# Graph attention hops: head rows loaded as a broadcast, scores spread by a bf16 product, tail scores added on the vector engine

## What is computed

```python
head, tail = (edge_index[0], edge_index[1])          # src, dst
rel_e = relation_emb[edge_type]
def agg(emb):
    a_input = jnp.concatenate([emb[head], emb[tail]], axis=-1)
    h = a_input @ fc_w.T + fc_b
    e = jnp.sum(h * rel_e, axis=-1)
    e = jnp.where(e > 0, e, LEAKY_SLOPE * e)          # slope 0.2
    m = jax.ops.segment_max(e, head, num_segments=N)
    ex = jnp.exp(e - m[head])
    denom = jax.ops.segment_sum(ex, head, num_segments=N)
    w = ex / denom[head]
    agg_emb = jax.ops.segment_sum(emb[tail] * w[:, None], head, num_segments=N)
    return agg_emb + emb
for _ in range(2):
    emb = agg(emb)
    nrm = jnp.sqrt(jnp.sum(emb * emb, axis=-1, keepdims=True))
    emb = emb / jnp.maximum(nrm, EPS)
```

## Time and profile before

| | us |
|---|---|
| median of 3 runs | 8037.34 |
| lowest and highest | 8023.26, 8038.31 |
| the profiled execution | 8036.36 |
| its span, first to last instruction | 8034.5 |
| POOL busy | 5792.3 (72%) |
| PE busy | 5700.0 (71%) |
| DVE busy | 4755.5 (59%) |
| ACT busy | 2380.1 (30%) |

### The profile page before, as it was taken

The page is one execution under the profiler, slowest core; times in us unless marked ns, Lnnn a source line. Parts: engine busy times, 40 slices in busy tenths (PEclk is TensorE's granted clock), DMA queues, the critical chain, the costliest instruction groups (busy, mean ns, idle before and its releaser), DMA issues. The chain is left out here.

```text
span 8034.5 us, 180792 instructions
## 1 busy us (share of the span) xinstructions
PE 5700.0 (71%) x46174; PEld 3902.5 (49%) x46175; DVE 4755.5 (59%) x24755; ACT 2380.1 (30%) x4713; POOL 5792.3 (72%) x5647
## 2 busy tenths in 40 slices
PE   0991699999001477778777767777777777588885
PEld 0110111111000377667677766777767667466664
DVE  6898655555001466666666666666666666555555
ACT  2000000000000244454444444545454445122221
POOL 0888877777777577777777747777777777277775
PEclk9995899999555687887888877887787888588888
DMA  2992577886001211212211221111212122233332
GB/s 68 307 309 63 151 244 244 244 244 212 4 4 21 62 53 53 53 53 53 53 53 53 53 48 53 53 53 53 53 53 53 53 53 53 34 69 69 69 68 55
DMA packets 375221, 721.44 MB, mean 90 GB/s; under 512 B 210770, under 2 KB 259945, under 8 KB 325885
## 3 DMA queue, kind: packets, MB, share of 16 engines
q10 hardware_dynamic: 76307, 411.51, 15.5%
q0 software_dynamic: 180560, 257.90, 14.7%
q1 hardware_dynamic: 118298, 51.38, 2.8%
HBM read 693.09 MB, written 19.44 MB: 89 GB/s over the span
## 5 line engine op out<-in xcount | busy, mean ns | idle before, releaser
L1108 POOL DMA_INDIRECT rows<-tab_d,stage_idx x3264 | 3090.3, 947 | 1100.8 <-issue 972.0
L214 POOL DMA_INDIRECT rec_d<-stage_rec,stage_row x1600 | 1955.4, 1222 | 673.1 <-issue 664.6
L424 PE MATMUL ps_gate<-ring,h_sb 128*1 128x512 f32 x3072 | 1486.3, 592 | 0.2 <-issue 0.2
L1150 PE MATMUL ps_x<-a_split,hot_t 128*128 x9792 | 577.8, 198 | 782.2 <-DMA rows<-tab_d,stage_idx 780.6
L1252 DVE SCALAR_TENSOR_TENSOR picked<-iota_f,typ_e,ps_x 128x50 f32<-128x50 f32 x3264 | 679.8, 264 | 685.6 <-PE ps_x L1153 680.5
L1161 PEld LDWEIGHTS ps_g<-rows,prob 128*128 128x128 f32 x6528 | 1070.3, 235 | 9.7 <-ACT prob L1196 8.5
L1161 PE MATMUL ps_g<-rows,prob 128*128 128x65 f32 x6528 | 1022.0, 310 | 2.7 <-ACT prob L1196 2.7
L1452 POOL DMA_INDIRECT y_rows<-y_d,stage_src x768 | 735.6, 958 | 368.6 <-issue 218.9
L1150 PEld LDWEIGHTS ps_x<-a_split,hot_t 128*128 128x128 bf16 x9792 | 464.0, 104 | 1014.1 <-issue 967.3
L1220 DVE CUSTOM_DVE_ANT_0 masked<-lower,ps_s 128x512 f32<-128x512 bf16 x816 | 561.7, 688 | 550.2 <-ACT lower L1190 420.9
L1188 ACT ACTIVATE hot_t<-ps_hot 128x512 bf16<-128x512 bf16 x816 | 487.1, 597 | 1271.8 <-PE ps_hot L1141 1258.4
(11 more groups left out here) (289 smaller groups left out, 7822.9 us busy)
## 6 DMA issues: line engine op xcount, KB each, us to landing
ring<-w_ih ACTq DMA_DIRECT2D x192, 1024.0 KB
ring<-w_hh ACTq DMA_DIRECT2D x192, 1024.0 KB
rows<-tab_d,stage_idx POOLq DMA_INDIRECT x3264
rec_e<-list_lo_d SPq DMA_DIRECT2D x216, 128.0 KB
rec_d<-stage_rec,stage_row POOLq DMA_INDIRECT x1600
y_rows<-y_d,stage_src POOLq DMA_INDIRECT x768
rec_d<-blank ACTq DMA_DIRECT2D x1, 3584.0 KB, 32.5
rec_e<-rec_d SPq DMA_DIRECT2D x1, 3584.0 KB, 11.2
```

Source lines behind the costliest of these rows:

```text
L214: pool.indirect_dma_start(out=rec_d, out_offset=bass.IndirectOffsetOnAxis(ap=stage_row[:, h, j:j + 1], axis=0), in_=stage_rec[:, h, j, :], ...
L424: mm = pe.matmul(ps_gate[:, s, :], lhsT=h_sb[:, kc:kc + 1], rhs=ring[:, pc % RING, q, :], start=(kc == 0), stop=(kc == KC - 1))
L1108: pool.indirect_dma_start(out=rows[:, h * 4 + g, k, :], out_offset=None, in_=tab_d[hop], in_offset=bass.IndirectOffsetOnAxis(ap=stage_idx[ ...
L1150: pe.matmul(ps_x[:, p, k * R:(k + 1) * R], lhsT=hot_t[:, p, k * P:(k + 1) * P], rhs=a_split[:, ds(bb, 1), j, :].rearrange("p a r -> p (a r)"),
```

## The change

All of it is in the hops and in what feeds them.

- **Head rows.** The position of each edge's head in its block, `lo`, is stored in device memory as bf16, one row of 512 per group (`lo_d`; new in the block of stage 2: an ACT copy `lo_rows` and one DMA). In a hop SP loads each group's row, broadcast to 128 partitions (`lo_wide`, 128 KB). DVE compares it with the partition's number: one instruction of 512 columns gives `hot_t`, another gives `lower`. The four `hot` instructions, PE's `turn_hot` and both ACT copies go.
- **Scores spread.** DVE splits each score in three bf16 parts in a zero-filled tile of 128 columns (`s_parts`). PE turns it (one bf16 transpose), ACT copies 128 columns (`s_rows`), and PE multiplies with constants `pick_k`, four bf16 products, in place of four f32 transposes.
- **Tail scores.** PE's f32 product L1153 goes. DVE adds `ps_x` and the tail scores in `rows` (`x_sum`, 200 columns), and `picked` reads `x_sum`. Now DVE, and not PE's `scores`, waits for `rows`.
- **Running maximum.** `m_old` is copied first and is the start value of the maximum; the factor for new sums is 1, so `acc` is updated by one instruction.
- **Lags** are 1, 2, 3 and 4 in place of 1, 2 and 3. `PER_GROUP` counts DVE's own waits, 12 for 8.
- In stage 2 `lo_e` is turned where `only_lo` was; `node_a` is replaced by `part_f` in the last stage.

```diff
@@ stage 2
-                sp.wait_ge(kept_rdy, CHUNKS // 2)
+                sp.wait_ge(kept_rdy, CHUNKS // 2 + 1)
+                sp.dma_start(lo_d.rearrange("g (k e) -> (g k) e", k=KT).rearrange("(c t) e -> t c e", t=P), lo_rows[:]
+                             ).then_inc(list_st, 16)
                 sp.dma_start(tile_d[0:T1].rearrange("(c p) e -> p c e", p=P), by_tile[:].rearrange("p c v e -> p c (v e)")
                              ).then_inc(tile_st, 16)
...
-                dve.scalar_tensor_tensor(out=only_lo[:], in0=rec_e[:, :, 3], scalar=-float(B_LO), in1=rec_e[:, :, 0],
-                                         op0=ALU.mult, op1=ALU.add).then_inc(to_turn, 1)
+                dve.tensor_copy(lo_e[:], rec_e[:, :, 0]).then_inc(to_turn, 1)
...
+                for k in range(KT):
+                    link(dve.tensor_copy(pick_k[:, k, :], ident_f[:, k:k + 1].broadcast_to([P, P])))
+                for j in range(1, 3):
+                    for k in range(KT):
+                        c = j * KT + k
+                        link(dve.tensor_tensor(pick_k[:, k, :], pick_k[:, k, :],
+                                               ident_f[:, c:c + 1].broadcast_to([P, P]), ALU.add))
...
+                act.wait_ge(kept_rdy, CHUNKS // 2)
+                act.activation(lo_rows[:], by_tile[:, :, 0, :], ACT.Copy).then_inc(kept_rdy, 1)
@@ hop, SP
+                        def head_rows(g, u):
+                            wait_tick(sp, tick, lo_in, g * 16)
+                            wait(sp, lower_rdy, g - 7)
+                            sp.dma_start(lo_wide[:, u % 8, :], lo_d[ds(g, 1), :].broadcast_to([P, GE])).then_inc(lo_in, 16)
+
+                        def round_of(it, last=False):
+                            for u in range(8):
+                                if not last or u + LO_AHEAD < 8:
+                                    head_rows(it * 8 + u + LO_AHEAD, u + LO_AHEAD)
+                                if not last and u % 4 == 3:
+                                    half(it + 1, u // 4)
@@ hop, PE
+                        def turn_scores(g, p):
+                            wait(pe, score_rdy, g + 1)
+                            wait(pe, s_kept, g)
+                            pe.transpose(ps_turn[:, 0:P], s_parts[:, p].rearrange("p j k -> p (j k)"), ident_b[:]
+                                         ).then_inc(s_turned, 1)
...
-                                mm = pe.transpose(ps_s[:, p, k * P:(k + 1) * P],
-                                                  score[:, p, k:k + 1].broadcast_to([P, P]), ident_f[:])
+                                mm = pe.matmul(ps_s[:, p, k * P:(k + 1) * P], lhsT=pick_k[:, k, :], rhs=s_rows[:, p, :],
+                                               start=True, stop=True)
...
                         def scores(g, p, u, bb):
-                            wait(pe, landed[u], (g - u) * 8 + 64)
...
-                            mm = pe.matmul(ps_x[:, p, 0:KT * R], lhsT=ident_f[:], rhs=rows[:, u, :, SC:SC + R],
-                                           start=False, stop=True, skip_group_check=True)
@@ hop, ACT
-                                act.activation(hot_t[:, p, :], ps_hot[:, 0:GE], ACT.Copy).then_inc(hot_t_rdy, 1)
-                                act.activation(lower[:, p, :], ps_hot[:, 0:GE], ACT.Copy, bias=-BIG, scale=BIG
-                                               ).then_inc(lower_rdy, 1)
+                                act.activation(s_rows[:, q, :], ps_turn[:, 0:P], ACT.Copy).then_inc(s_kept, 1)
@@ hop, DVE
+                                link(dve.tensor_scalar(m_old[:, p:p + 1], m_of, 1.0, None, ALU.mult))
...
+                                wait(dve, lo_in, i * 16 + 16)
+                                wait(dve, x_rdy, i - 1)
+                                dve.tensor_scalar(hot_t[:, u % 2, :], lo_wide[:, u % 8, :], part_f[:], None, ALU.is_equal
+                                                  ).then_inc(hot_t_rdy, 1)
+                                dve.tensor_scalar(lower[:, u % 4, :], lo_wide[:, u % 8, :], part_f[:], -BIG,
+                                                  ALU.not_equal, ALU.mult).then_inc(lower_rdy, 1)
...
+                                wait(dve, landed[(u - 1) % 8], (g - (u - 1) % 8) * 8 + 64)
                                 wait(dve, x_rdy, g + 1)
+                                link(dve.tensor_tensor(x_sum[:], ps_x[:, q, 0:KT * R].rearrange("p (k r) -> p k r", k=KT),
+                                                       rows[:, (u - 1) % 8, :, SC:SC + R], ALU.add))
```

207 lines of the change are left out of this document (96 added, 111 removed).

## The result

The changed kernel takes **8066.15 us** in the median (8064.8 to 8068.7), the kernel before 8037.5 beside it: ratio 1.0038, 95% interval 1.0026 to 1.005. It is slower by 29 us, more than the 0.2% that can be told from no change. The forecast was 8058 (8032 to 8150), with "slower" at 0.50 and "the same" at 0.46.

A forecast was written before the change was run, and what follows sets the result against it. POOL's back-to-back gathers, one group per 5.0 us, were taken to bound the hops. The sum was 8036.4 + 18 (gathers) + 3 (stage 2) + 1 (ends of the hops) = 8058 us, range 8032 to 8150.

The forecast's parts named there:

- POOL as the bound: In the hops, POOL issues indirect gathers without a pause, one group per 5.0 us, and everything else follows it.
- PE's and ACT's gain at nothing: In the hops, some 1.4 us less PE work per group and less ACT copying, costed at nothing under POOL's cover.
- rival 3: In the hops, a step passes 5.0 us through mis-sized DVE work or PE's lower clock: 8216 us at 5.2; chance 0.12.
- PE less busy: Sign of being right: in the hops PE and ACT are less busy, at an unchanged pace; no size given.
- DVE's step of 4.4 us: In the hops, DVE's instructions for one group sum to 4.4 us, under POOL's 5.0; 4.7 if `lower` is slow.
- busy for 4.2 to 4.6 us a group: Sign of being right: DVE's busy time per group in the hops, while it still waits for `rows`.
- POOL's gathers, +18 us: In the hops, DVE's wide comparisons and picks hold gathers, net 5.5 ns each over 3264; bounds nothing to +82 us.
- Rival 1: In the hops, DVE's new instructions all miss POOL's gathers, so not slower: 8040 us; chance 0.35.
- rival 2: In the hops, each group's gathers meet one comparison for 0.1 us, locked in the bad place: 8122 us; chance 0.10.
- The reading of L538 in the prediction: L538, a DVE instruction with two inputs, left a scatter at its usual 1.19 us; if picks behaved so, 8050 us.
- Stage 2, +3 us: In stage 2, a shorter cast saves 1.5 us; the new copy, issue and transfer add: net +2.5, from -1 to +6.
- The ends of the hops, +1 us: From the last `ps_x` to the last `acc`, work removed and added nets +0.5 us a hop, from -2 to +2.

The follow-up runs named there:

- second run: The changed kernel, unaltered, measured again beside the kernel before on another chip where POOL's gathers stand back to back: 8059.6 us, ratio 1.0035.

## Why the prediction came out as it did

**POOL as the bound, and PE's and ACT's gain at nothing: right.** The gathers stay back to back, and with three quarters of them gone both kernels run much faster. PE's clock fell to its lower level for the whole of the hops (0.81 to 0.51), as rival 3 held possible, and the step stayed under 5.0 us all the same. Of the signs named for being right, "PE less busy" holds only just, 308.6 us for 312.5 in 400.

**DVE's step of 4.4 us: right**, 4.40 in the step shown and 4.39 in the mean with POOL out of the way. But the sign "busy for 4.2 to 4.6 us a group" failed: it is 3.78. The sum ran from start to start, with the handovers in it, and the sign called the same figure busy time. Of the parts, `x_sum` is 0.36 (0.41 in the sum), the doubled operation of `lower` 0.34 and not 0.69, and `masked` with `m_old` 0.75. Rival 3, a step over 5.0, is out where POOL is the bound.

**POOL's gathers, +18 us: right, with 15.3 measured.** The mechanism and its 0.12 us were read from the earlier trace rows and hold in the hops. The mean is 951.4 ns for 952 forecast, POOL's period 2049.4 / 408 = 5.02 us for 5.03. The two terms were sized 9.5 us for the comparisons, net, and 8.5 for the picks; measured are 10.6 and 5.8. Rival 1 (they all miss) and rival 2 (locked, 82 us) are out. A gather meets a wide comparison 137 times in 816 groups, one in six, not far from what chance would give for two openings of 0.14 us (the longest hold) in a gather's period of 1.25: 0.22.

The picks were the doubtful part: the Trainium skill, "GPSIMD Engine Reference", section Specifications, counts an instruction with two SBUF inputs among those that contend with POOL, and the earlier trace rows showed one that did not. Here 252 gathers of the changed kernel end with a pick, and none does once the picks' second input is in PSUM: the trace agrees with the page. The reading of L538 in the prediction was wrong, and the trace of before shows why. L538 meets 126 scatters. 96 of them begin 0.03 us or less after it did, as in the earlier trace rows (740.77 and 740.78), and the other 30 find less than 0.07 us of it left; none falls where a gather was held above. L569 meets 23 scatters, all at least 0.15 us after its own start and with over 0.13 us left, and all 23 are held, for what was left less 0.13 us within 5 ns. So L538 is no exception.

**Stage 2, +3 us: +1.8.** `lo_e` comes first and the copy takes 1.70 us (1.8 costed), the issue 0.41.

**The ends of the hops, +1 us: wrong, +6.6.** This step failed. It compared the chain of the last group alone, what goes and what is added on it, and took the chain as free of others. But the added stage leaves one more group's pass, 3.5 us, to be done on PE and ACT behind the last `score`. Of the chain that it did look at, it took too little off: that got 2.0 us an end shorter, where the sum has 0.5 longer. The trace of before had the durations (the earlier trace rows has `ps_g` at 1.81 and `ps_p` at 1.06); what was missing was to count which groups are still in the pipeline when the last rows land. The remaining 3.6 of the 6.6 us are no part of that mechanism: 2.4 of stops beside packets of instructions and 1.2 of the clock, for which the sum had no term.

**The tail of the kernel, not forecast: +3.6.** Three quarters of it stand in one row of the last stage, in code that nobody changed:

```profile
8032.24 1.76 DVE L1339 TENSOR_TENSOR x<-acc,var 128x1536 f32<-128x1536 f32 x1 [2.70 <-issue]
```

DVE waits for nothing there, and an 8 KB packet of the queue that brings instructions moves in that gap (at 8030.5 us, the next at 8032.9). In the kernel before, the same instruction stands at 8003.59 without a gap, and the packets of this queue come at 8024.1 and later, after DVE's last instruction. The changed kernel has the gap, 2.7 us, in its second run too. It is the same kind of stop as in the ends of the hops. That the changed length of the code moved the place at which it is fetched is what this suggests; it was not tried.

The sum would have been 8036.4 + 15.3 + 1.8 + 6.6 + 3.6 and 2.5 us of stretches that the edit does not touch: 8066. The forecast was 8 us short: 5.6 at the ends of the hops, 3.6 in the tail and 2.5 in the untouched stretches, less 2.7 for the holds and 1.2 for stage 2, which came out shorter than forecast. With the holds and stage 2 alone, the terms that the sum got about right, the kernel would have been 17 us slower, at the edge of the 0.2% that can be told. That "slower" came out clear of it is in part luck: it takes terms that the sum mis-sized or left out.

## What to carry to other kernels

When one engine is the bound, ask of an edit what it does to that engine's own instructions, and only then what it saves. Here a wide bf16 comparison, or an instruction with both inputs in SBUF, on an engine with a quarter of its time free, costs the bounding POOL some 85 ns (a pick 23) whenever a gather starts in the right stretch behind its start. When a row seems to show that an instruction does not contend, look whether the two really met: set the starts beside each other, over all its instances. A stage more in a software pipeline cost nothing in its middle and one pass of the slowest engines, 3.5 us, at every drain; count, for the end of a loop, the groups that are still in the pipeline behind the last one. Before a few us at such an end are put down to the edit, look for stops with no releaser in both traces. And measure on more than one chip where transfers are near the bound.
